# Reading a tile's expert at its use on ScalarE and VectorE, instead of four experts at the head of a round, in a cross-attention and mixture-of-experts kernel

## What is computed

```python
x = x + xattn(layernorm(x), ctx, Wq, Wkv, Wproj, bproj)      # softmax(q k^T / 8) v, then Wproj
h = layernorm(x)                                             # 3584 tokens
probs = softmax(h @ gate_w)                                  # 8 experts
top_p, top_i = top_k(probs, 2);  top_p /= sum(top_p)
for e in 8:  out[e] = (silu(h @ Wg[e]) * (h @ Wu[e])) @ Wd[e]    # 256 -> 512 -> 256
x = x + sum over the two chosen experts of out * top_p
```

## Time and profile before

| | us |
|---|---|
| median of three runs | 1512.29 |
| profiled execution, its own time | 1513.29 |
| its span | 1511.5 |
| TensorE busy | 1448.6 (96%) |
| VectorE busy | 1027.1 (68%) |
| ScalarE busy | 813.4 (54%) |
| GpSimd busy | 555.9 (37%) |

### The profile page before, as it was taken

The page is one execution under the profiler, slowest core; times in us unless marked ns, Lnnn a source line. Parts: engine busy times, 40 slices in busy tenths (PEclk is TensorE's granted clock), DMA queues, the critical chain, the costliest instruction groups (busy, mean ns, idle before and its releaser), DMA issues. The chain is left out here.

```text
span 1511.5 us, 38193 instructions
## 1 busy us (share of the span) xinstructions
PE 1448.6 (96%) x12134; PEld 1285.2 (85%) x12135; DVE 1027.1 (68%) x2664; ACT 813.4 (54%) x2159; POOL 555.9 (37%) x641
## 2 busy tenths in 40 slices
PE   6999999999999999999999999999997899999996
PEld 5888889888888889898988889898885788888885
DVE  5667777776777677776777677767768675555554
ACT  4555555555555555555555555555555554445543
POOL 3523334343334343333434333434253532222222
PEclk9999999999999999999999999999998999999999
DMA  9222222222223222222222222221035332233222
GB/s 262 75 66 67 77 67 73 66 71 71 72 73 93 83 71 71 66 78 65 74 65 71 71 72 77 79 76 50 27 124 217 59 58 49 49 51 52 49 49 25
DMA packets 101107, 113.82 MB, mean 75 GB/s; under 512 B 17244, under 2 KB 88140, under 8 KB 101068
## 3 DMA queue, kind: packets, MB, share of 16 engines
q1 hardware_dynamic: 87900, 94.33, 20.3%
q0 software_dynamic: 12144, 15.66, 6.4%
q10 hardware_dynamic: 1024, 3.34, 0.7%
HBM read 61.37 MB, written 51.93 MB: 75 GB/s over the span
## 5 line engine op out<-in xcount | busy, mean ns | idle before, releaser
L851 ACT ACTIVATE prob<-bank,neg_max 112x375 f32<-112x375 f32 x512 | 299.0, 589 | 134.5 <-DVE neg_max L1212 134.5
L1212 DVE TENSOR_REDUCE neg_max<-bank 112x1 f32<-112x375 f32 x512 | 243.8, 539 | 14.4 <-PE bank L1454 14.3
L1464 PE MATMUL bank<-ident,prob 112*125 112x112 f32 x1536 | 214.5, 273 | 2.7 <-ACT prob L851 2.4
L1464 PEld LDWEIGHTS bank<-ident,prob 112*125 112x125 f32 x1536 | 195.9, 188 | 13.8 <-ACT prob L851 5.0
L1362 PE MATMUL bank<-Wgu,hT_h 128*128 x504 | 167.9, 415 | 25.2 <-DVE hT_l L1278 25.2
L786 POOL DMA_INDIRECT out<-y_out,dest_now x63 | 100.8, 1600 | 223.7 <-ACT y_out L960 175.5
L1488 PE MATMUL bank<-probT,V 125*64 125x112 f32 x3072 | 175.5, 263 | 2.6 <-DVE probT L1218 1.8
L1000 DVE TENSOR_TENSOR K_l<-bank,K_h 128x376 fp32r<-128x376 f32 x256 | 140.4, 550 | 52.5 <-ACT K_h L811 45.6
L1488 PEld LDWEIGHTS bank<-probT,V 125*64 125x64 f32 x3072 | 148.1, 137 | 29.1 <-issue 25.9
L990 DVE COPY V<-bank 125x512 f32<-125x512 f32 x96 | 66.4, 692 | 139.2 <-PE bank L1426 136.2
L809 ACT COPY V<-bank 125x512 f32<-125x512 f32 x96 | 56.4, 588 | 181.8 <-PE bank L1426 179.3
(11 more groups left out here) (209 smaller groups left out, 3890.9 us busy)
## 6 DMA issues: line engine op xcount, KB each, us to landing
bins<-pad_rows SPq DMA_DIRECT2D x29, 1032.0 KB, 5.8
inv_rows<-sums SPq DMA_DIRECT2D x126, 128.0 KB, 2.9
h_in<-bins SPq DMA_DIRECT2D x63, 129.0 KB, 2.5
Wgu<-in_L_ffn_gate_up_w SPq DMA_DIRECT2D x6, 1024.0 KB, 7.4
y_sb<-in_ctx SPq DMA_DIRECT2D x32, 187.5 KB, 2.7
y_sb<-in_ctx SPq DMA_DIRECT2D x62, 93.8 KB, 2.7
x_sb<-in_x SPq DMA_DIRECT2D x16, 224.0 KB, 2.8
x_res<-in_x SPq DMA_DIRECT2D x32, 112.0 KB, 2.5
```

The source lines that it names most:

```text
L851: nc.scalar.activation(prob[:, j, :], S_ps[j][0:LQ, 0:LKV], ACT.Exp, bias=neg_max[:, j:j + 1], accum_out=row_sum[:, head // HB, head % HB: ...
L1212: nc.vector.tensor_reduce(neg_max[:, j:j + 1], S_ps[j][0:LQ, 0:LKV], AX.X, ALU.max, negate=True).then_inc(max_done, 1)
L1464: last = nc.tensor.transpose(S_ps[j][0:KR, t * LQ:t * LQ + LQ], prob[:, j, t * KR:t * KR + KR], ident[0:LQ, 0:LQ])
```

## The change

On ScalarE and on VectorE the read of four experts at the head of a round goes; in its place a single entry is read within each iteration, where the down weights are indexed: on ScalarE right before L954 and behind its wait for `down_made`, on VectorE right before L1325 and behind its wait for `wd_hi`. In the written-out rounds the address is a constant, in the loop it is computed from the round's register. ScalarE's wait for the first part of the table moves from ahead of round 0 to behind the first silu. The last batch's `open_gates` on ScalarE moves from the end of iteration 5 to iteration 6, behind L954 and ahead of `y_out`. TensorE's own reads (L1627) stay.

```diff
 # ScalarE
-            def experts_from(i):
-                c = 4 * i + 1
+            def expert_of(t):
                 return nc.values_load_multi_w_load_instructions(
-                    tile_expert[0:1, c:c + 4] if known(i) else tile_expert[0:1, bass.ds(c, 4)],
-                    engines=(mybir.EngineType.Activation,), min_val=0, max_val=E - 1)[1]
+                    tile_expert[0:1, t + 1:t + 2] if known(t) else tile_expert[0:1, bass.ds(t + 1, 1)],
+                    engines=(mybir.EngineType.Activation,), min_val=0, max_val=E - 1)[1][0]
 
             def four_tiles(i):
-                if known(i) and i == 0:
-                    act.wait_ge(plan, N_PLAN1)
-                experts = experts_from(i)
...
                         if known(t) and t == 0:
+                            act.wait_ge(plan, N_PLAN1)
                             act.wait_ge(proj_made, B)
...
                         if not known(t) or t >= 2:
                             act.wait_ge(down_made, t - 1)
-                        nc.scalar.copy(down_parts[k % 2][:, 0], Wd[:, experts[k]]).then_inc(wd_hi, 1)
+                        nc.scalar.copy(down_parts[k % 2][:, 0], Wd[:, expert_of(t)]).then_inc(wd_hi, 1)
+                    if known(t) and t == 6:
+                        open_gates(B - 1, C_ps)
                     if there(t - 1, NT):
...
-                    if known(t) and t == 5:
-                        open_gates(B - 1, C_ps)
 # VectorE: the same expert_of(t), with engines=(mybir.EngineType.DVE,)
             def four_tiles(i):
-                experts = experts_from(i)
...
                         dve.wait_ge(wd_hi, t + 1)
-                        nc.vector.tensor_tensor(down_parts[k % 2][:, 1], Wd[:, experts[k]],
+                        nc.vector.tensor_tensor(down_parts[k % 2][:, 1], Wd[:, expert_of(t)],
                                                 down_parts[k % 2][:, 0].bitcast(F32), ALU.subtract).then_inc(wd_lo, 1)
```

More of the change, by code:

```diff
@@ L1298, in _, with expert_of @@
                 lo_of_expert(e)
-            def experts_from(i):
-                c = 4 * i + 1
+            def expert_of(t):
                 return nc.values_load_multi_w_load_instructions(
-                    tile_expert[0:1, c:c + 4] if known(i) else tile_expert[0:1, bass.ds(c, 4)],
-                    engines=(mybir.EngineType.DVE,), min_val=0, max_val=E - 1)[1]
+                    tile_expert[0:1, t + 1:t + 2] if known(t) else tile_expert[0:1, bass.ds(t + 1, 1)],
+                    engines=(mybir.EngineType.DVE,), min_val=0, max_val=E - 1)[1][0]
             def four_tiles(i):
-                experts = experts_from(i)
                 for k in range(4):
```

## The result

The changed kernel takes 1487.62 us (median of four runs, 1486.97 to 1491.06), beside it the kernel before 1512.48 (1512.16 to 1513.98). The ratio is 0.9838, with 0.9821 to 0.9855 as its 95% interval. The gain is 24.9 us; 18.5 were forecast. The lower end of the predicted range was 1489, 1.4 us above the result: the gain came out larger than was predicted. The profiled execution of the changed kernel took 1491.06 us, its span is 1489.3. In the table further down one execution of ScalarE alone, the one of 1513.65 us, was in a slower state than the rest and is not in its ratio.

The account below looks back on a forecast made before the run. TensorE was taken to bound the kernel, with breaks at round heads. The sum 20.8 + 0.1 - 2.4 = 18.5 us, off the median 1512.29, gave 1494 us; forecast bounds 1488.5 to 1502, range 1489 to 1503.5.

Parts of the forecast that it names:

- What bounds the kernel: Expert stage: TensorE with breaks; it sat idle 17.9 us behind VectorE's hT_l, ScalarE's hT_h 21.3 us for its own sequencer.
- The prize of 20.8 us, rounds 4 to 15: Iterations 15 to 61: 12 heads cost 1.73 us each above the floor of 4.89 us an iteration, 20.8 us in all.
- The branch and its register step at a head: Before hT_h at a round's head: 0.3 us of cover, costed at nothing; without cover at most 0.4 us a round, 5 us.
- The cost of the reads per tile: Single reads of 0.91 us on ScalarE and 1.27 on VectorE delay hT_l: 2.4 us over 47 tiles, bounds 0 and 7.5.
- the +0.1 of the first three rounds: Balance of TensorE's waits for hT_l won against later routing steps in the first three rounds: +0.1 us, bounds -2 and +3.
- h: Distance of hT_l's start from U, the start of the iteration's up product: 5.39 to 6.04 us, 5.85 taken.
- the edge of 5.82: hT_l is due 5.82 us after the up product's start U; the path was forecast to end on both sides of that.
- The 6.0 us set against the 6.9: First three rounds: 6.9 us of TensorE's waits for hT_l to win, against five routing iterations longer by 1.2 us, 6.0.
- The gates, up to 0.7 us: Moving the last batch's gates from iteration 5 behind L954 gains up to 0.7 us, counted within the 6.9.
- Reads paid per tile: Rival, 8%: ScalarE's read waits for the queued silu, period 5.46 us, 27 us lost, kernel slower at 1520 us.
- the law of that rival: Path over two iterations to hT_l: two periods are h + 0.56 + 3.5 us; the kernel is slower from h = 6.6.
- The stores: Rival, 4%: output DMAs one behind the other, 4.7 us against 4.89, set the pace; no change, 1512 us.

Follow-up runs that it names:

- ScalarE alone: The kernel before with only ScalarE reading a single entry at its use; VectorE's read of four and the gates stay: 1492.07 us, ratio 0.9851.
- the second run of the changed kernel: The changed kernel run again with nothing altered: 1487.23 us, ratio 0.9824 to the kernel before.
- VectorE alone: The kernel before with only VectorE reading a single entry at its use; ScalarE's read of four stays at the head: 1512.82 us, ratio 0.9992.
- four at use: The changed kernel, but each read at its use on ScalarE and VectorE takes four entries and uses the first: 1541.71 us, ratio 1.0167.
- the shift: The kernel before with its table written three entries further on, so a round's four entries begin at 4i + 4: 1502.07 us, ratio 0.9934.

## Why the prediction was right and wrong

**What bounds the kernel: right.** TensorE with breaks at the heads, made by ScalarE's sequencer. The two experiments with one engine each show it: all of the steady gain with ScalarE alone, nothing with VectorE alone.

**The prize of 20.8 us, rounds 4 to 15: right.** Measured 20.2; the floor was 4.903 and not 4.89 in this execution, 46 x 0.013 = 0.6. In the second run of the changed kernel (224.71) it is 21.0.

**The branch and its register step at a head, cost nothing: right.** Iterations 16, 20, ... 60 are as long as the others.

**The cost of the reads per tile: the step that failed.** The sum took 0.91 and 1.27 us for a single-entry read from the earlier trace rows, whose reads are of four entries. It scaled the register steps down to one value, but not the read. Measured are 0.28 and 0.31. The forecast gain fell short by this price in two terms: the 2.4 us of the steady part, which are nothing, and the +0.1 of the first three rounds, which is +5.1 and lies above the term's own bound of +3. The mechanism, short reads bare at the head and covered or cheap at the use, was right. The rest of the path was right but for a slip: the parts of the copy's start add up to U + 1.73 and not 1.77, which changes nothing. With h at its upper end, 6.04, and the two reads corrected by 0.63 and 0.97, hT_l could start at U + 4.44. In the timeline after, the low part starts at U + 3.28 and the next instruction could start 1.15 behind it: U + 4.43. Forecast for the low part was U + 4.24 to 4.89, a gap of 1.5 to 1.9 behind the copy; it is 0.85. So instead of standing on the edge of 5.82 the path has 1.4 us of spare, and hT_l starts at U + 5.30, when ScalarE's hT_h lets it. The term of 2.4 us is nothing.

The trace of before had the row that would have given the price away. TensorE reads the same table, four entries in a round and two at another place in it. Its sequencer instructions, first in 1244 to 1248.5 us, then in 1248.5 to 1254:

```profile
L1627 PEldq SEQ_ASSERT  x4: 18/18/18, 1246.2 to 1247.1; - x4
L1627 PEldq TENSOR_LOAD <-tile_expert x1: 337/337/337, 1245.6 to 1245.6; - x1
```

```profile
L1627 PEldq SEQ_ASSERT  x2: 18/18/18, 1253.1 to 1253.4; - x2
L1627 PEldq TENSOR_LOAD <-tile_expert x1: 538/538/538, 1252.3 to 1252.3; - x1
```

The asserts count the entries. Four cost 0.34 us and two 0.54: a read's duration is neither fixed nor simply the number of its entries, and a bound for one entry had to reach down to 0.34 at least. The prediction looked at the rows of the two engines concerned alone and gave its prices no such bound. The sentence on the Trainium skill (DMA: Bandwidth & Descriptors, Latency and other measured facts), that a tensor_load has a floor of about 600 ns, was set apart there as a price by which nothing would be late. That outcome came, but the floor isn't one here: single reads take 0.28 and 0.31, and 1265.29 above is one of four at 0.31. Its advice to take four at a time fits here only four aligned entries, which take 0.31 us where one takes 0.28; four unaligned ones at use made the kernel 25 us slower than before the change.

**The first three rounds, +0.1 us: wrong in size.** Measured +5.1. The balance itself wasn't worked out to its end: 6.9 - 6.0 is 0.9, and the 0.8 between that and 0.1 was given for the first output DMA without a row. The larger cause is the same misread duration: 1.7 us of added path in each of five routing tiles assumed 0.97 + 0.29 for the read and 0.45 for the copy, of which 0.31 + 0.40 and nothing are real, and TensorE spares 0.54 of the remaining 0.71. The 6.0 us set against the 6.9 shrink to some 5 x 0.17 = 0.9. That the length of the reads decides there is shown by the kernels with more entries at use: 70.67 us from U1 to U15 with one, 73.11 with two, 77.20 with three, 89.12 with four. Iteration by iteration the trace gives 4.5 us won at the heads (4, 8 and 12), 1.8 in iterations 6 and 7, and 1.3 lost in 2, 3, 10 and 11. The wait that went, on VectorE in iteration 4 (timeline, before and after):

```profile
1184.66 0.42 DVE L1278 TENSOR_TENSOR hT_l<-bank,hT_h 128x256 fp32r<-128x256 f32 x1 [2.00 <-issue]
```

```profile
1186.08 0.16 DVE L1137 SCALAR_TENSOR_TENSOR bin_row<-top_f,rank 112x2 int32<-112x2 f32 x1
1186.15 0.42 DVE L1275 TENSOR_TENSOR hT_l<-bank,hT_h 128x256 fp32r<-128x256 f32 x1
```

There, unlike at the later heads, it was VectorE's read that was bare, behind the routing steps. TensorE's waits for hT_l in 1166 to 1232 us fell from 6.9 us to

```profile
PE bank L1357 <- DVE hT_l L1275: 1.3, 3, 0.6
```

The heads of round 1 and 2 need VectorE's part, that of round 3 ScalarE's: with ScalarE alone iteration 4 keeps its 2.49 us, with VectorE alone iteration 12 keeps 1.53. So VectorE's part, worth nothing by itself, is worth something beside ScalarE's. By itself it shortens iterations 4 and 8 by 1.9 and 0.6 us, but 2, 3, 7, 9 and 11 are longer by as much together. With both reads and without the gates 74.19 falls to 72.58, and the ratio from 0.9851 to 0.9834, though these intervals overlap. Iterations 8 to 10 were to be longer: 10 and 11 are, by 0.3 us each (5.16 and 5.31 us), but 8 is shorter by 1.0, since it held a head. Iteration 3, not forecast to be longer, is so by 0.5 us (5.19 to 5.65). There VectorE waits for the landing of the first output DMA before it may write `dest_now`, and its product of silu and up, which TensorE needs, stands behind that (timeline after):

```profile
1183.36 0.15 DVE L1283 CAST dest_now<-h_in 128x1 int32<-128x1 f32 x1 [2.77 <-DMA out<-y_out,dest_now]
```

The landing came at U1 + 12.9 us instead of 12.3 (1183.33 and 1179.94), the delay of the first output DMA that the prediction named for iteration 1.

**The gates, up to 0.7 us: open in size.** The late gates of iterations 6 and 7 are gone, 1.9 to 2.1 us in the traces, nothing that the times can tell. For the drain of 1.38 us that the Trainium skill (ScalarE: Activation LUTs, What ACT_TABLE_LOAD costs) adds to a table load, this is ScalarE's timeline after:

```profile
1196.90 1.05 ACT L951 CAST down_even<-Wd 128x1024 fp32r x1
1197.97 1.28 ACT L862 ACT_TABLE_LOAD   x1
1199.26 0.27 ACT L862 ACTIVATE gates<-bank,neg_top 112x8 f32<-112x8 f32 x1
```

The load starts 0.02 us behind the copy's end and the Exp 0.01 behind the load's: 1.28 us and no drain. The 1 us that the low end of the sum kept for it wasn't needed.

**The rivals.** Reads paid per tile made the kernel with four at use slower, by the mechanism and the law of that rival; single reads are too short for it, and ScalarE's doesn't wait for the queued silu. The stores didn't set the pace, since TensorE waits for nothing in the steady part, but they came as near as can be: from issue to landing they take 4.0 us in the middle and 4.6 at most now, against the 3.8 and 4.1 of the earlier trace rows, and with the 0.8 or 0.9 to the next issue that is the whole 4.90. The waits of GpSimd in the result section say the same. At the end of the chain:

```profile
1473.10 3.76 DMA out<-y_out,dest_now
...
1477.74 3.84 DMA out<-y_out,dest_now
```

From one to the next it is 4.64 us there, 0.26 under the iteration's 4.90. Whoever makes TensorE's iteration shorter will find them next. Whether their landings would then get shorter again isn't shown.

With the two terms corrected, 20.8 + 5.1 - 0, the prediction's own sum gives 25.9, and 1486.4 us. The first 5.1 is the measured value put in, so this shows that nothing else is missing from the sum, not that it could have been forecast.

## What to carry to other kernels

In this kernel a sequencer's read of a register value costs only where its engine has nothing queued: behind a semaphore's wait it stands bare, behind queued work it is free, so look at what is in flight on that engine and not at the read's length alone. Before a price is taken from the nearest row, see whether that row does the same amount of work as the new instruction, and look for other engines that execute the same instruction at other sizes. And the releaser in a wait's row is the last link; undo one engine's part at a time to see whose time it is.

## What the runs showed of the hardware

- **A TENSOR_LOAD's duration goes by the entries and their alignment.** Of this int32 table, in the steady part one entry takes 0.28 us on ScalarE and 0.31 on VectorE, two 0.49 and 0.53 to 0.85, three 0.70 and 0.74 to 1.04, four 0.91 and 0.96 to 1.27: 0.21 us for each further entry on ScalarE. Four entries that begin at a multiple of four take 0.31, and 0.35 to 0.43 on VectorE, little more than one; two and three have no such short form. TensorE shows the same: 0.34 for four aligned, 0.54 for two, 1.0 to 1.3 for four after the shift. The kernel before paid the long form at each head, by a table that begins at entry 1.
- **ScalarE's sequencer runs ahead of the engine.** The single read starts 0.45 us before the silu that precedes it in the program (1256.2 to 1256.65) and the copy behind it starts as early as without a read.
- **The stores of `y_out` land later when they have no rest.** From issue to landing the median is 3.8 us in the kernel before, with rest at each head, and 4.0 in the changed kernel; why was not found.
- **Each value read costs register steps besides,** 0.15 us on ScalarE and 0.19 on VectorE with an assert and gaps: 0.23 and 0.28 us a value. Where four were read for the use of one, that is 0.7 to 0.8 us more.
- **The granted clock fell to 0.50 (1.2 GHz) for some 3 us** behind two breaks of TensorE in one profiled execution, and not behind a break as long in another. What decides it was not found.
